# A graph attention kernel: 44 of 49 node tiles normalised and stored inside the last twelve turns of the edge pass

## The reference, cut to what matters

```python
# 6250 nodes, 206250 edges sorted by dst, width 96, 8 heads of 12
x = layernorm(x + L0(x, src, dst))               # mean and max aggregation, two batch norms
K, Q, V = x @ Wk + bk, x @ Wq + bq, x @ Wv + bv  # L1, per node
Ee = edge_attr @ We + be                         # per edge
score = exp(clip(sum_over_head(K[src] * Q[dst] / sqrt(12) * Ee), -5, 5))
wV = segment_sum(V[src] * score, dst)
Z = segment_sum(score, dst)
x = layernorm(x + wV / (Z + 1e-6))               # the node tiles of this change
```

## Time and profile before

| | |
|---|---|
| time, median of 3 runs | 4199.84 us (4194.13 to 4200.12) |
| the profiled execution: time, span | 4203.19 us, 4201.5 us |
| mean granted clock of TensorE in it | 0.983 |
| busy: PE, DVE, ACT, POOL | 3754.9, 2322.0, 1501.6, 3089.7 us |

### The profile page before, as it was taken

How to read it: one execution, slowest core, us unless ns; L and a number is a source line. 1 busy time by engine, 2 the same in 40 slices (tenths; PEclk the granted TensorE clock), 3 DMA queues, 4 the chain that set the end, 5 groups by cost and what they waited for, 6 DMA issues and landing times.

```text
span 4201.5 us, 106452 instructions
## 1 busy us (share of the span) xinstructions
PE 3754.9 (89%) x30382; PEld 3249.7 (77%) x30382; DVE 2322.0 (55%) x5891; ACT 1501.6 (36%) x4201; POOL 3089.7 (74%) x3253
## 2 busy tenths in 40 slices
PE   7988888888888888888799999999999999999996
PEld 6777777777777777777588888888888888888885
DVE  5555555555555555555645555555555555555556
ACT  3333333333333333333433333333333333333333
POOL 7777777777777777777367777777777777777774
PEclk9999999999999999999789999999999999999997
DMA  3111111111111111111144444444444444444442
GB/s 92 40 39 39 39 39 39 39 39 39 39 39 39 39 39 39 39 39 39 42 117 118 118 118 118 118 118 117 118 118 118 117 118 118 118 118 118 117 118 71
DMA packets 208677, 330.89 MB, mean 79 GB/s; under 512 B 72877, under 2 KB 156520, under 8 KB 208648
## 3 DMA queue, kind: packets, MB, share of 16 engines
q0 software_dynamic: 129040, 238.05, 23.0%
q1 hardware_dynamic: 79608, 92.48, 7.5%
HBM read 323.08 MB, written 7.22 MB: 79 GB/s over the span
## 4 chain that ended last, share of the span: by engine, by line
POOL 43%; issue 33%; DMA 9%; PE 9%; DVE 4%; POOLq 1%; ACT 1%; DVEq 0%; ACTq 0%; SPq 0%
POOL kvg L413 42%; DMA kvg<-kv_table,idx 7%; DMA kvg<-in_x_dram,idx 2%; PE bank L1041 1%; DVE prod L927 1%; DVE msg L951 1%; PE bank L1052 1%; PE bank L1202 1%; PE bank L1101 1%; PE bank L1216 1%; PE bank L1084 1%; PE bank L1211 1%; PE bank L1233 1%; DVE S L661 1%; PE bank L1043 1%
## 5 line engine op out<-in xcount | busy, mean ns | idle before, releaser
L413 POOL DMA_INDIRECT kvg<-kv_table,idx x1613 | 1529.8, 948 | 506.2 <-issue 471.1
L413 POOL DMA_INDIRECT kvg<-in_x_dram,idx x1613 | 1531.8, 950 | 497.0 <-issue 484.8
L678 DVE TENSOR_TENSOR_SCAN scan<-keepC,scan,bank 96x512 f32<-96x512 bf16 x404 | 515.5, 1276 | 498.2 <-PE bank L1052 497.0
L1041 PE MATMUL bank<-ident,kvg 128*96 128x128 f32 x3232 | 452.1, 283 | 228.7 <-DMA kvg<-in_x_dram,idx 219.0
L1041 PEld LDWEIGHTS bank<-ident,kvg 128*96 128x96 f32 x3232 | 367.2, 164 | 292.4 <-DMA kvg<-in_x_dram,idx 217.7
L1202 PE MATMUL bank<-ident,S 128*64 128x128 f32 x3232 | 433.2, 277 | 140.9 <-DVE S L661 138.9
L920 DVE TENSOR_TENSOR prod<-kvg,bank 128x384 f32<-128x384 f32 x404 | 223.8, 554 | 588.5 <-DMA kvg<-kv_table,idx 426.7
L1202 PEld LDWEIGHTS bank<-ident,S 128*64 128x64 f32 x3232 | 345.4, 137 | 230.2 <-issue 230.2
L1101 PEld LDWEIGHTS bank<-S,scanE 128*96 128x96 f32 x3232 | 339.7, 165 | 217.9 <-issue 215.5
L492 ACT COPY scanE<-bank 128x384 f32<-128x384 f32 x404 | 193.7, 479 | 752.4 <-PE bank L1093 752.4
L1216 PE MATMUL bank<-qwin,scan 64*128 64x96 f32 x3232 | 457.8, 282 | 0.0
(11 more groups left out here) (155 smaller groups left out, 5088.0 us busy)
## 6 DMA issues: line engine op xcount, KB each, us to landing
ea<-in_edge_attr_dram SPq DMA_DIRECT2D x402, 192.0 KB
kvg<-in_x_dram,idx POOLq DMA_INDIRECT x1613, 2.5
kvg<-kv_table,idx POOLq DMA_INDIRECT x1613
kv_table<-stage SPq DMA_DIRECT2D x6, 672.0 KB, 3.3
xN<-in_x_dram SPq DMA_DIRECT2D x6, 336.0 KB, 3.2
out_dram<-xN SPq DMA_DIRECT2D x6, 336.0 KB
src_all<-in_src_groups_dram SPq DMA_DIRECT2D x1, 804.0 KB
stage<-in_dst_groups_dram SPq DMA_DIRECT2D x1, 804.0 KB
```

The costliest lines, as they stand in the source:

```text
L413: pool.indirect_dma_start(out=to[:, r, j, :], out_offset=None, in_=table, in_offset=bass.IndirectOffsetOnAxis(ap=idx[:, r, j:j + 1], axis= ...
L678: dve.tensor_tensor_scan(out=scan[:, r % 2, :], data0=keepC[:, r % 2, :], data1=bank[2 + r % 2][0:D, :], initial=scan[:, (r + 1) % 2, GE - ...
L1041: pe.matmul(bank[0][0:D, j:GE:J], xg[:, r, j, 0:D], ident[:, :], start=True, stop=True)
```

## The change

The second pass's last twelve turns (from turn `T0` = 89) are written out instead of looped. In them, group 356 + t also carries node tile t, for t below 44: PE transposes the tile's `acc` columns into spare columns of the bank of the queries, DVE copies them to `raw`, and four tiles (a quad) later divides, adds `xN` and takes statistics, each at the end of a step; eight tiles (a pair of quads) share a root on ACT and a store. The results stand in `y`, which lies where the key/value table was staged; so DVE waits for that table's store before the pass. Five tiles remain for the end, all in one round. `row_stats` and `row_scale` are the old statistics and scale for these tiles; `late_step` numbers the steps from turn 89 on (`at`). The old `last_norm` stays for the general path only. POOL has no part in the new path.

```diff
+T0 = 89
+QUADS = 11
+DONE = QUADS * 4
+LASTS = NT - DONE
...
+        def late_tile(i, r):
+
+            t = (i - T0) * R + r if isinstance(i, int) else -1
+            return t if t < DONE else -1
...
+        LAST = ((DONE, DONE + 3), (DONE + 3, NT))
...
+            def store_rows(t0, t1):
+                sp.wait_ge(s_yfin, t1)
+                sp.dma_start(out[t0 * P:t1 * P, :].rearrange("(t p) c -> p t c", p=P), y[:, t0:t1, :]
+                             ).then_inc(s_yout, 16)
+
+            with sp.Fori(1, T0 + 5) as i:
                 for r in range(R):
                     sp.wait_ge(s_T, freed(i, r, R))
                     load_group(i, r)
+            for i in range(T0 + 5, FULL // R):
+                for r in range(R):
+                    sp.wait_ge(s_T, freed(i, r, R))
+                    load_group(i, r)
+                if (i - T0) % 2 == 0:
+                    pair = (i - T0 - 6) // 2
+                    store_rows(pair * 8, pair * 8 + 8)
...
+            for pair in range(3, QUADS // 2):
+                store_rows(pair * 8, pair * 8 + 8)
+            store_rows(DONE - 4, DONE)
+            flag = load_flag(sp)
+            store_rows(DONE, NT - 1)
+            sp.wait_ge(s_yfin, NT)
+            sp.dma_start(out[NFULL * P:N, :], y[0:NTAIL, NFULL, :]).then_inc(s_yout, 16)
+            sp.wait_ge(s_yout, 16 * (QUADS // 2 + 3))
...
+                    late_rows(late_step(i, r))
+
+            def root(t0, t1, quads):
+                act.wait_ge(s_ymv, quads)
+                act.activation(yr[:, t0:t1], ymv[:, t0:t1, 1], ACT.Sqrt, bias=eps_col[:, 0:1]).then_inc(s_ysd, 1)
+
+            def normalize_rows(t0, t1, n):
+                act.wait_ge(s_yb, n)
+                for t in range(t0, t1):
+                    act.activation(y[:, t, :], y[:, t, :], ACT.Identity, bias=yb[:, t:t + 1], scale=yr[:, t:t + 1]
+                                   ).then_inc(s_yfin, 1)
+
+            def late_rows(at):
+                pair, part = (at - 13) // 8, (at - 15) % 8
+                if at >= 13 and (at - 13) % 8 == 0 and pair < QUADS // 2:
+                    root(pair * 8, pair * 8 + 8, pair * 2 + 2)
+                pair = (at - 15) // 8
+                if at >= 15 and part < 4 and pair < QUADS // 2:
+                    normalize_rows(pair * 8 + part * 2, pair * 8 + part * 2 + 2, pair + 1)
+
+            pipeline(act, turn2, 2, unrolled=TURNS - T0)
...
                 def products_q(r):
                     b = r % 2
+                    t = late_tile(i, r)
+                    if t >= 0:
+                        dve.tensor_copy(raw[:, t // 4 % 2, t % 4, :], bank[4 + b][:, J * D:J * D + DMSG]
+                                        ).then_inc(s_raw, 1)
...
+            def shares(q):
+
+                dve.wait_ge(s_raw, 4 * q + 4)
+                dve.tensor_scalar_add(ynz[:, quad(q), :], raw[:, q % 2, :, D:DMSG], 1e-6).then_inc(s_ynz, 1)
+                dve.wait_ge(s_ynz, 2 * q + 1)
+                dve.reciprocal(ynz[:, quad(q), :], ynz[:, quad(q), :]).then_inc(s_ynz, 1)
+
+            def residual(q):
+                dve.wait_ge(s_ynz, 2 * q + 2)
+                dve.tensor_tensor(y[:, quad(q), :].rearrange("p k (h d) -> p k h d", d=HD),
+                                  raw[:, q % 2, :, 0:D].rearrange("p k (h d) -> p k h d", d=HD),
+                                  ynz[:, quad(q), :].unsqueeze(3).to_broadcast([P, 4, H, HD]),
+                                  ALU.mult).then_inc(s_y, 1)
+                dve.wait_ge(s_y, 2 * q + 1)
+                dve.tensor_tensor(y[:, quad(q), :], y[:, quad(q), :], xN[:, quad(q), :], ALU.add).then_inc(s_y, 1)
...
+            def late_rows(at):
+                if at % 4 == 2 and 0 <= at - 6 < QUADS * 4:
+                    shares((at - 6) // 4)
+                if at % 4 == 3 and 0 <= at - 7 < QUADS * 4:
+                    residual((at - 7) // 4)
+                if at % 4 == 0 and 0 <= at - 8 < QUADS * 4:
+                    q = (at - 8) // 4
+                    row_stats(range(q * 4, q * 4 + 4), 2 * q + 2, q + 1)
+                if at >= 14 and (at - 14) % 8 == 0 and (at - 14) // 8 < QUADS // 2:
+                    pair = (at - 14) // 8
+                    row_scale(pair * 8, pair * 8 + 8, pair + 1)
...
+            dve.wait_ge(s_kvtab, 16 * (NK + 1))
+            pipeline(dve, turn2, 4, unrolled=TURNS - T0)
+            row_scale(DONE - 4, DONE, QUADS // 2 + 1)
...
                     pe.wait_ge(s_qc, ready(i, r))
+                    t = late_tile(i, r)
+                    if t >= 0:
+                        pe.wait_ge(s_acc2, freed(i, r, 8))
+                        pe.transpose(bank[4 + b][:, J * D:J * D + DMSG], acc[0:DMSG, 0, t * P:(t + 1) * P],
+                                     ident[0:DMSG, 0:DMSG])
...
+            for h, (t0, t1) in enumerate(LAST):
+                for t in range(t0, t1):
+                    last = pe.transpose(bank[h][:, (t - t0) * DMSG:(t - t0 + 1) * DMSG], acc[0:DMSG, 0, t * P:(t + 1) * P],
+                                        ident[0:DMSG, 0:DMSG])
+                last.then_inc(s_rows, 1)
```

More of the change, by code:

```diff
@@ L228, in wait_past, with pipeline @@
                 eng.wait_ge(s, value)
-        def pipeline(eng, turn, lag, turns=TURNS, per=R, peel=0, between=()):
+        def pipeline(eng, turn, lag, turns=TURNS, per=R, peel=0, between=(), unrolled=0):
             peel = max(peel, -(-lag // per))
@@ L238, in pipeline @@
                     work()
-            if peel < turns:
-                with eng.Fori(peel, turns) as i:
+            last = turns - unrolled
+            if peel < last:
+                with eng.Fori(peel, last) as i:
                     turn(i, range(per), lambda r: True)
+            for p in range(last, turns):
+                turn(p, range(per), lambda r: True)
             turn(turns, range(lag), lambda r: r < 0)
@@ L373, in _, with store @@
                     sp.dma_start(ea[0:EC, 0, 0, :], edge_attr[bass.ds(c * EC, EC), :]).then_inc(s_ends2, 16)
[L375 to L384, removed]
+                def store(i, tiles):
+                    sp.wait_ge(s_fin, i * K7 + K7)
+                    sp.dma_start(out[bass.ds(i * KC, tiles * P), :].rearrange("(t p) c -> p t c", p=P),
+                                 xN[:, bass.ds(i * K7, tiles), :]).then_inc(s_out, 16)
+                with sp.Fori(0, NK - 1) as i:
+                    store(i, K7)
+                store(NK - 1, K7 - 1)
+                sp.dma_start(out[NFULL * P:N, :], xN[0:NTAIL, NFULL, :]).then_inc(s_out, 16)
+                sp.wait_ge(s_out, 16 * (NK + 1))
         @block.gpsimd
@@ L584, in turn2 @@
                         exp(r - 2)
-            pipeline(act, turn2, 2)
+                    late_rows(late_step(i, r))
[15 more added lines that the diff above has]
+            pipeline(act, turn2, 2, unrolled=TURNS - T0)
+            for at in range(late_step(TURNS, 2), 8 * (QUADS // 2) + 11):
+                late_rows(at)
+            root(DONE - 4, DONE, QUADS)
+            normalize_rows(DONE - 4, DONE, QUADS // 2 + 1)
+            root(DONE, NT, QUADS + 1)
+            normalize_rows(DONE, NT, QUADS // 2 + 2)
             with irregular(act):
@@ new lines, in row_stats, with row_scale @@
+            def row_stats(tiles, added, n):
+                dve.wait_ge(s_y, added)
+                for t in tiles:
+                    last = dve.bn_stats(yst[:, t, :], y[:, t, :])
+                last.then_inc(s_yst, 1)
+                dve.wait_ge(s_yst, n)
+                for t in tiles:
+                    last = dve.bn_aggr(ymv[:, t, :], yst[:, t, :])
+                last.then_inc(s_ymv, 1)
+            def row_scale(t0, t1, n):
+                dve.wait_ge(s_ysd, n)
+                dve.reciprocal(yr[:, t0:t1], yr[:, t0:t1]).then_inc(s_yr, 1)
+                dve.wait_ge(s_yr, n)
+                dve.scalar_tensor_tensor(out=yb[:, t0:t1], in0=ymv[:, t0:t1, 0], scalar=-1.0, in1=yr[:, t0:t1],
+                                         op0=ALU.mult, op1=ALU.mult).then_inc(s_yb, 1)
@@ new lines, in _ @@
+            dve.wait_ge(s_ynz, 2 * QUADS + 2)
+            dve.reciprocal(ynz[:, DONE:NT, :], ynz[:, DONE:NT, :]).then_inc(s_ynz, 1)
+            dve.wait_ge(s_ynz, 2 * QUADS + 3)
+            for h, (t0, t1) in enumerate(LAST):
+                rows = bank[h][:, 0:(t1 - t0) * DMSG].rearrange("p (k c) -> p k c", c=DMSG)
+                dve.tensor_tensor(y[:, t0:t1, :].rearrange("p k (h d) -> p k h d", d=HD),
+                                  rows[:, :, 0:D].rearrange("p k (h d) -> p k h d", d=HD),
+                                  ynz[:, t0:t1, :].unsqueeze(3).to_broadcast([P, t1 - t0, H, HD]),
+                                  ALU.mult).then_inc(s_y, 1)
```

153 lines of the change are left out of this document (89 added, 64 removed).

## The result

The changed kernel took 4168.12 us (median of 4, 4164.19 to 4178.03) beside 4198.49 for the kernel before: ratio 0.9933, 95% interval 0.9913 to 0.9952. In a later session it was 0.9924 (0.9909 to 0.9938). The forecast was 4174.5 (4167 to 4184). Its sum was made for the profiled execution: 4177.8 forecast, 4178.03 measured, span 4176.3. That execution is the slowest of the four; on the medians the gain is 30.4 us, in the later session some 32 (26 to 38), where the sum has 25.4. So the close match holds for one pair of profiles, and the sum has to be taken apart.

The account below looks back on a forecast made before the run. POOL's own gather issue, 5.01 us a group, was taken to pace the second pass, with the node loop behind it; -30.6 + 2.3 + 0.4 + 2.5 = -25.4, so 4203.2 becomes 4177.8, on the median 4174.5 (4167 to 4184).

Parts of the forecast that it names:

- The tail: Node loop behind the last window addition: five of 49 tiles left, 42.1 us becomes 11.5, so -30.6.
- The drain: End of the second pass: the last quad's product step and statistics stand before the last two `prod`, +2.3 us.
- The 0.4 for two transposes: End of the second pass: two of PE's added transposes fall into a half-clock stretch, +0.4 us.
- The gathers: Second pass: DVE operations with two SBUF inputs hold up POOL gathers caught at an exposed instant, +2.5 us, bounds 0 and 8.
- Twelve turns become straight code: nothing.: Second pass's last turns: writing them out costs nothing, as POOL kept its pace in the first pass's six such turns.
- A granted clock below 1.00 before 4118: Sign in the profile after, second pass: PE's clock below 1.00 before 4118 us would show the forecast wrong.
- gathers that wait for `msg`: Sign in the profile after, second pass: POOL gathers waiting for a message would show the forecast wrong.
- The wait for the key/value table: Start of the second pass: DVE's first one-hot moves 3.4 us later, hidden with 2.3 us to spare.
- the first one: Rival, end of the second pass: PE's added work keeps its clock from falling; -30 us, 4170; chance 0.15.
- lock and stores bite: Rival, second pass: gathers and DVE hold each other up and stores delay landings; -16 us, 4184; chance 0.17.
- Slower: Rival, changed turns: PE falls to 1.2 GHz and stays, 2.9 us more a group; +44 us, 4244; chance 0.04.
- the late steps in DVE's hole: Second pass: late node steps, none over 1.2 us, fit DVE's 1.46 us wait before `prod`, so they are free.

Follow-up runs that it names:

- the drain order: The changed kernel with the last quad's product step and statistics moved two steps later, behind the last two `prod`; ratio 0.9926 to the kernel before.
- straight code alone: The kernel before with only the second pass's last 12 turns written out, no late work, ratio 0.9996; with 24 turns written out, 0.9994.
- the stores behind: The changed kernel with all finished-row stores behind the last edge load, ratio 0.9926; two further variants combine this with other edits, 0.9931 and 0.9937.
- the hoisted order: The changed kernel with DVE's one-hot and message put ahead of `prod` for the whole second pass; ratio 0.9923 to the kernel before.

## Why the prediction was right, step by step

- **The tail, -30.6.** Right, -31.4, and the same in every kernel that has it (10.7 to 10.9 us). The rest is the last store, 3.3 us where the earlier trace rows gave 4.0.
- **The drain, +2.3.** Right, +1.8 to +2.5 by the rows and 2.0 undone by the drain order. It isn't always paid in full: in the second profile of the changed kernel, without the hole at the edge tail, the drain took 11.3, 0.8 above the 10.5 with straight code alone, where the same `prod` waits 1.37 us for its landing and so covers part of the step. The granted clock in these two drains was nearly the same, 0.66 and 0.64. The 0.4 for two transposes can't be told apart from the rest.
- **The gathers, +2.5.** The mechanism is right, the size isn't: 1.5 us, in the other two profiles of the changed kernel 1.4 and 1.1. The exposed instant and the 0.82 behind the operation's end hold in every case read; in the second passes of the four traces without late work no gather exceeded 0.975 us (the changed kernel has one of 1.00 in its looped part, at 3379). But many quads lose only 0.04 to 0.07, because the operation ends just behind the instant. I had put each at 0.25, and one gather in sixteen at 1.1 us or more; it was four of some 180. The Trainium skill, "SBUF — State Buffer", section "Who interferes with whom", lets the later of the two block; of that the rows show POOL's side, counted from the instant and not from the start (in the third profile a product that began 0.04 us behind a gather's start still held it up, to 1409 ns), while L1081 never took more than 620 ns (median 559), and L1076 not more than 542.
- **"Twelve turns become straight code: nothing."** By itself right (0.9996). The reason given, that POOL kept its pace in the first pass's straight turns, was too thin: the code has to be fetched while the gathers land, and it makes some 5 of 40 landings late. The Trainium skill, "Runtime: NRT & Kernel Launch", section "Instruction fetch mechanics", describes refills in blocks of 16 KiB on a queue of the sequencer's own and calls their cost mostly hidden. The packets of q8 agree (0.48 MB in 29), those of q14 are half as large (0.20 MB in 25); the time agrees too (0.9996), the landings of the gathers don't.
- **"A granted clock below 1.00 before 4118" and "gathers that wait for `msg`"** were named as what would show the forecast wrong, and both came: the larger of the missing terms. Where the fall lasted 20 us POOL was held 3 to 5 us, twelve times out of twelve before the drain (2.7 to 4.8); in passes whose falls last 14 us or less, 0.9 us at most in all. In the changed kernel it is 6.6 to 9.4 us an execution. That PE's time matters so soon could be read before: the earlier trace rows leave out that 27 of the 96 `prod` in that stretch waited for PE's L1216 (45.9 us) and not for a landing. The sum of the first profile held all the same because POOL ran 5.8 us faster by pace, and that is luck. The medians gained 5 to 7 us more than the sum. Before has long falls at its edge tail too (4.0 us held and a drain of 15.4 in its second profile); whether they make up the difference isn't shown.
- **The wait for the key/value table, "hidden, with 2.3 to spare".** Right for the fifth group: the first message was over at 2142.7 (forecast 2142.4). But the second message came 26.0 us behind the first gather, where the sixth group wanted it at 25.0, and POOL waited 2.12 us there, 2.06 in the third profile. In both the clock stayed at 0.50 until 17 us behind the first gather; in the second profile it was back after 9 and POOL didn't wait. The second profile of before, without the table wait, loses 3.6 us at the same place with a clock of 0.50 from 6 to 30 us. So this wait goes with the clock, and the share of the table wait in it isn't separated.
- **The rivals.** The clock did fall at the edge tail (0.60 over 4125 to 4150), so the first one, 4170 on its own ground, isn't what happened in the first profile; the second and third lack that hole and have drains of 11.3 and 11.2, as that rival has it, but why isn't shown. Of "lock and stores bite" the lock came to 1.5 instead of 8; the stores do delay landings. "Slower" priced a group at 1.2 GHz at 2.9 us; two falls of 20 us, some eight groups, held POOL for 6.6 to 9.4 us in all.
- **Costed at nothing and right:** the copy of a tile, the late steps in DVE's hole, the store waits (PE never waits for an edge load there), and ten more table loads before the end, where eleven were expected. PE's waits at the one-hot fell as expected: 16.1 us from 3895 to 4118 before, 5.4 now.

What stays open: why one fall lasts 20 us and the next 10 behind like waits, and so whether late work (B) makes the long ones likelier; and why the medians gain more than the sum. Both kernels with straight code alone had no long fall before the edge tail, the changed kernel one or two in each of three profiles; but four variants with all the late work had none either, three of them those with the stores behind, and one profile each is too little.

## What to carry to other kernels

Cut both spans at the same events before believing a sum: here a total within 0.3 us hid a missing +8 and an unearned -6. Where the bound is an engine whose transfers must land in time, price what straight code and stores add to the DMA traffic, and ask how long an engine downstream may run slow before the bound one waits: here falls of 10 to 14 us cost 0.9 at most in a whole pass and one of 20 cost 3 to 5. And a work step moved ahead of the last items of a pipeline is paid in the drain however well it was hidden before, in full where those items wait for the engine that does it (1.8 to 2.5 here), in part where they wait for a landing (0.8).

## What the runs showed of the hardware, unexpected

- POOL's gather has two paces, one for a whole execution: 944 and 946 ns in the two passes, or 947 and 949, with the same code and on the same chip. Over 3226 gathers 2.4 ns each are 7.7 us, 0.2% of the time. The medians of VectorE's and ScalarE's frequent operations differ by 2 ns at most, either way.
- A packet of 8 or 16 KB of instructions, 0.3 to 1.8 us long on its DMA engine, went, in 14 of 52 cases with straight code alone, with a group's landing 2.6 to 3.3 us behind its last gather, where 2.1 to 2.2 are usual. A store of 384 KB issued 0.5 to 1.0 us before that gather's end did so ten times of ten (3.0 to 3.4), at other moments not once by itself.
- Single waits of TensorE of 1.0 to 3.4 us, in stretches where it is otherwise busy for 93%, were followed, though not each time, by 1.2 GHz for 3 to 20 us; in the hoisted order even waits of 0.46 and 0.17, 15 us behind one of 0.98, were.
